# Adapters in float16 halves, turned by DMA and normalised in two fused VectorE passes

## The reference

```python
x = x + cross_attention(x, f)        # 16 heads of 32, keys/values from x, plus one "self" score per query
x = x + softmax((f' + bias) @ f.T) @ f         # layer 1: one head over 512 features
# layer 2, per sample one of 10 adapters
h = relu(x @ W1 + b1); y = x + h @ W2 + b2
x = x + (y - mean(y)) * rsqrt(var(y) + 1e-5) * gamma + beta
# layer 3, per sample one of 4 low-rank pairs
x = x + (x @ A.T) @ B.T + emb
```

## Time and profile before

| | |
|---|---|
| time, median of 3 runs | 1299.4 us (1297.53 to 1302.03) |
| the profiled execution | 1299.96 us; its span 1298.2 us; mean granted PE clock 0.991 |
| busy share of the span | PE 97%, DVE 66%, ACT 65%, POOL 38% |
| one sample | 156.2 us from one mid stage to the next |

### The profile page before, as it was taken

One profiled execution on the slowest core, in us unless ns is written; L12 is line 12 of the kernel. 1 busy time (PEld: TensorE's weight loads), 2 busy tenths in 40 slices (PEclk: granted clock), 3 DMA queues, 4 the chain that ended last, 5 costly groups with the idle time before them and its releaser, 6 DMA issues.

```text
span 1298.2 us, 19231 instructions
## 1 busy us (share of the span) xinstructions
PE 1258.6 (97%) x6697; PEld 523.2 (40%) x6697; DVE 860.6 (66%) x1561; ACT 848.3 (65%) x1795; POOL 489.5 (38%) x428
## 2 busy tenths in 40 slices
PE   7899999999999999999999999999999999999996
PEld 4332454325543344433544245442454324543243
DVE  5976449764697547974389743886449855597544
ACT  4898349873598636985379753888439873598631
POOL 6414344143632246321553416514244143532024
PEclk9999999999999999999999999999999999999996
DMA  6303532135223152242521334213442136222020
GB/s 216 72 16 108 108 69 70 56 91 109 50 65 106 53 98 63 52 125 47 97 62 50 116 74 82 55 53 108 93 77 62 43 98 127 52 66 89 5 33 33
DMA packets 156142, 98.85 MB, mean 76 GB/s; under 512 B 107338, under 2 KB 130182, under 8 KB 156046
## 3 DMA queue, kind: packets, MB, share of 16 engines
q1 hardware_dynamic: 155984, 97.61, 31.1%
q10 hardware_dynamic: 62, 0.01, 0.0%
HBM read 40.81 MB, written 8.40 MB: 38 GB/s over the span
## 4 chain that ended last, share of the span: by engine, by line
PE 70%; DVE 14%; ACT 13%; issue 2%; POOL 1%; ACTq 0%; POOLq 0%; DVEq 0%
PE bank L476 24%; PE banks L476 13%; PE banks L1441 8%; PE bank L1457 8%; DVE nmx L1093 7%; ACT banks L814 6%; PE banks L1376 4%; ACT big L865 4%; PE bank L1278 3%; PE bank L1404 2%; PE bank L1409 2%; PE bank L1431 2%; PE bank L1467 1%; DVE y L1051 1%; ACT bank L894 1%
## 5 line engine op out<-in xcount | busy, mean ns | idle before, releaser
L814 ACT ACTIVATE banks<-banks,nmx 128x512 f32<-128x512 f32 x512 | 341.7, 685 | 41.6 <-DVE nmx L1093 39.4
L1093 DVE TENSOR_REDUCE nmx<-banks 128x1 f32<-128x512 f32 x512 | 328.8, 686 | 16.9 <-PE banks L1376 16.0
L865 ACT ACTIVATE big<-banks 128x1024 f32<-128x1024 f32 x256 | 248.0, 1021 | 54.4 <-PE banks L1441 53.4
L476 PE MATMUL bank<-fT,w_hi 128*128 128x512 f16 x768 | 255.7, 379 | 0.7 <-DVE fT L1007 0.6
L1376 PE MATMUL banks<-KQ 97*128 97x512 f16 x512 | 195.8, 382 | 11.0 <-ACT banks L814 10.8
L1441 PE MATMUL banks<-KQ 98*128 98x512 f16 x512 | 143.5, 383 | 3.6 <-ACT big L865 0.2
L476 PE MATMUL bank<-fT,w_lo 128*128 128x512 f16 x384 | 145.4, 379 | 0.0
L511 POOL TENSOR_TENSOR half<-qk,ones 128x512 f16<-128x512 f32 x64 | 66.7, 1042 | 206.4 <-ACT qk L796 197.9
L511 POOL TENSOR_TENSOR split<-tiles_in,ones 128x512 f16<-128x512 f32 x56 | 60.4, 1079 | 222.3 <-DMA xT<-split 206.2
L1457 PE MATMUL bank<-big,V 128*32 128x512 f32 x1024 | 136.4, 605 | 0.0
L586 POOL TENSOR_TENSOR x<-x,bo_rows 128x512 f32<-128x512 f32 x32 | 40.1, 1286 | 208.1 <-DMA x<-in_x_dram 208.1
(11 more groups left out here) (154 smaller groups left out, 1821.4 us busy)
## 6 DMA issues: line engine op xcount, KB each, us to landing
KQ<-half SPq DMA_DIRECT2D x384, 64.0 KB, 2.0
tiles_in<-in_x_dram SPq DMA_DIRECT2D x32, 256.0 KB, 7.7
x<-in_x_dram SPq DMA_DIRECT2D x8, 1024.0 KB, 5.9
out_dram<-x SPq DMA_DIRECT2D x32, 256.0 KB, 2.0
tiles_in<-in_fside_BxSxS_dram SPq DMA_DIRECT2D x28, 256.0 KB, 3.7
w<-in_L_cond_W_dram SPq DMA_DIRECT2D x16, 256.0 KB, 4.7
b2r<-in_L_cond_b_dram SPq DMA_DIRECT2D x8, 256.0 KB, 4.6
gr<-in_L_cond_gamma_dram SPq DMA_DIRECT2D x8, 256.0 KB, 5.5
```

The costliest lines, as they stand in the source:

```text
L476: mm = eng.matmul(out_ap, pairs[n][0], pairs[n][1], start=(first and n == 0), stop=(last and n == len(pairs) - 1))
L814: eng.activation(bank(step, i)[:, v, :], bank(step, i)[:, v, :], ACT.Exp, bias=nmx[:, t, h:h + 1], accum_out=esum[:, t, h:h + 1]).then_inc ...
L865: eng.activation(big[:, n % 2, 2 * u:2 * u + 2, :], bank(step)[:, :, :], ACT.Exp).then_inc(read(step), 1)
L1093: eng.tensor_reduce(nmx[:, t, h:h + 1], bank(step, i)[:, v, :], AX_X, ALU.max, negate=True).then_inc(max_done, 1)
```

## The change

Layers 2 and 3 are computed in float16 halves in place of float32. In the seven mid stages x1 is split into a high half (ACT) and a low half (DVE) and turned by SP's DMA transposes (steps `X2`, in place of `X2T`); after the normalisation POOL splits x3 (`X3`) and SP turns it (`T3`). `HID` and `LOW` then work on a pair of tiles (256 tokens): 12 and 8 float16 matmuls of 128x256. `LORA` is one float16 matmul. W1 is split by POOL in the attention stage (`split_w1`). The normalisation is two DVE operations for each tile: `U` (`centre`: (y - mean) times gamma) and `SCALE` (`scale`: times 1/sqrt, plus x1 + beta); POOL does no part of it but x1 + b2 and x1 + beta as before. y of all four tiles has room of its own (`tiles_in`), so that all `ADP` can run early. The table `at` gives the slots (entry n stands in slot 2n). After sample 7 the transposes by PE stay, with halves (ACT high, DVE low). The small tables are made earlier in the attention stage, on DVE.

```diff
@@ order_mid: the adapters' places @@
-        adapters = [("X2T", 0), None, ("HID", 0), None, ("ADP", 0), None, ("X2T", 1), ("SQ", 0), ("HID", 1), ("ADP", 1),
...
+        at = {2: [("HID", 0)], 3: [("ADP", 0)], 4: [("SQ", 0), ("ADP", 1)], 5: [("SQ", 1), ("HID", 1)],
+              6: [("U", 0), ("ADP", 2)], 7: [("U", 1), ("SQ", 2), ("ADP", 3)], 8: [("SQ", 3)], 9: [("U", 2)], 10: [("U", 3)],
+              11: [("SCALE", 0)], 12: [("SCALE", 1)], 14: [("X3", 0)], 15: [("X3", 1)], 16: [("SCALE", 2), ("T3", 0)],
+              17: [("SCALE", 3), ("X3", 2), ("T3", 1)], 18: [("X3", 3)], 21: [("T3", 2)], 22: [("T3", 3)],
+              24: [("LOW", 0)], 25: [("LORA", 0)], 27: [("LORA", 1)], 29: [("LOW", 1)], 31: [("LORA", 2)], 33: [("LORA", 3)]}
+        for n in range(NORM_PIECES):
+            at[8 + n // 2] += [("NORM", 0, n)]
+            at.setdefault(13 + n // 2, []).append(("NORM", 2, n))
...
-    out, later = [], {}
+    out, later = [("X2", t) for t in range(NT) if tail], {}
@@ POOL @@
-                    elif step[0] == "SCALE":
+                    elif step[0] == "X3":
                         t = step[1]
-                        eng.wait_ge(normed, i * NT + t + 1)
-                        eng.tensor_tensor(y[:, t % 2, :], y[:, t % 2, :], gr[:, :], ALU.mult).then_inc(scaled, 1)
-                        eng.wait_ge(scaled, i * NT + t + 1)
-                        eng.wait_ge(xg_done, i * NT + t + 1)
-                        eng.tensor_tensor(x1[:, t, :], y[:, t % 2, :], x1[:, t, :], ALU.add).then_inc(x3_done, 1)
+                        eng.wait_ge(x3_done, i * NT + t + 1)
+                        eng.wait_ge(x2t_in[t // 2], i * 32 + 32)
+                        split(p16[:, t, 0:S], p16[:, t, S:2 * S], x1[:, t, :], x3_hi, i * NT + t + 1, x3_lo)
@@ SP @@
+                    elif step[0] == "X2":
+                        t = step[1]
+                        eng.wait_ge(x2_lo, i * NT + t + 1)
+                        turn(aT2, t, p16[:, t, :], x2t_in[t // 2])
+                    elif step[0] == "T3":
+                        t = step[1]
+                        eng.wait_ge(x3_lo, i * NT + t + 1)
+                        turn(aT2, t, p16[:, t, :], x3t_in[t // 2])
@@ ACT @@
+                    elif kind == "X2":
+                        t = step[1]
+                        wait_read(eng, ("PV1", t), i)
+                        eng.activation(p16[:, t, 0:S], x1[:, t, :], ACT.Copy).then_inc(x2_hi, 1)
@@ DVE @@
+            def centre(t, i):
+
+                eng.wait_ge(sq_done, i * NT + t + 1)
+                eng.scalar_tensor_tensor(out=yb[:, t, :], in0=yb[:, t, :], scalar=st[:, t, 1:2], in1=gr[:, :],
+                                         op0=ALU.add, op1=ALU.mult).then_inc(normed, 1)
+
+            def scale(t, i):
+                eng.wait_ge(newton, i * (NT // 2 * NEWTON) + t // 2 * NEWTON + NEWTON)
+                eng.wait_ge(normed, i * NT + t + 1)
+                eng.wait_ge(xg_done, i * NT + t + 1)
+                eng.scalar_tensor_tensor(out=x1[:, t, :], in0=yb[:, t, :], scalar=st[:, t, 4:5], in1=x1[:, t, :],
+                                         op0=ALU.mult, op1=ALU.add).then_inc(x3_done, 1)
...
+                    elif kind == "X2":
+                        t = step[1]
+                        eng.wait_ge(x2_hi, i * NT + t + 1)
+                        eng.tensor_tensor(p16[:, t, S:2 * S], x1[:, t, :], p16[:, t, 0:S], ALU.subtract).then_inc(x2_lo, 1)
@@ PE @@
                     elif kind == "HID":
+                        at = tokens(step, head)
...
+                        if head:
+                            eng.wait_ge(x2t_in[step[1]], i * 32 + 32)
...
+                        hi_lo(eng, bank(step, i)[:, 0:at.stop - at.start], [(w1[:, 0, d, :], w1[:, 1, d, :]) for d in range(ND)],
+                              [(aT2[:, 0, d, at], aT2[:, 1, d, at]) for d in range(ND)]).then_inc(done(step, i), 1)
...
                     elif kind == "LOW":
+                        at = tokens(step, head)
+                        if head:
+                            eng.wait_ge(x3t_in[step[1]], i * 32 + 32)
```

More of the change, by code:

```diff
@@ L83, in order_mid @@
     if tail:
-        n0, n2 = ([("NORM", t, n) for n in range(NORM_PIECES)] for t in (0, 2))
-        adapters = [("X2T", 0), None, ("HID", 0), None, ("ADP", 0), None, ("X2T", 1), ("SQ", 0), ("HID", 1), ("ADP", 1),
[L86 to L92, removed]
+        at = {2: [("HID", 0)], 3: [("ADP", 0)], 4: [("SQ", 0), ("ADP", 1)], 5: [("SQ", 1), ("HID", 1)],
[3 rows of a table added]
+              24: [("LOW", 0)], 25: [("LORA", 0)], 27: [("LORA", 1)], 29: [("LOW", 1)], 31: [("LORA", 2)], 33: [("LORA", 3)]}
+        for n in range(NORM_PIECES):
+            at[8 + n // 2] += [("NORM", 0, n)]
+            at.setdefault(13 + n // 2, []).append(("NORM", 2, n))
+        adapters = [at.get(n, []) for n in range(max(at) + 1)]
     slots = (parts(("K", 0)) if tail else [("IN", NT), ("IN", NT + 1), *parts(("K", 0))[:2], ("IN", NT + 2), *parts(("K", 0))[2:4],
@@ L134, in order_mid @@
     assert rows and i >= max(later)
-    return out + [a for a in adapters if a] + ([] if sums else [("SROW",)])
+    return out + [a for each in adapters for a in each] + ([] if sums else [("SROW",)])
 OPEN = ((32, 26, 26, 26), (24, 24, 24, 24))
@@ L208, in order_last, with tokens @@
             + [("X2T", 0), ("HID", 0), ("X2T", 1), ("PV1", 2), ("ADP", 0), ("HID", 1), ("SQ", 0),
-               ("PV1", 3), ("ADP", 1), ("SQ", 1), ("X2T", 2)] + norm[0]
+               ("PV1", 3), ("ADP", 1), ("U", 0), ("SQ", 1), ("X2T", 2), ("U", 1)] + norm[0]
             + [("HID", 2), ("X2T", 3), ("SCALE", 0), ("HID", 3), ("X3T", 0), ("SCALE", 1), ("ADP", 2), ("LOW", 0),
-               ("X3T", 1), ("SQ", 2), ("ADP", 3), ("LOW", 1), ("SQ", 3)] + norm[2]
+               ("X3T", 1), ("SQ", 2), ("ADP", 3), ("LOW", 1), ("U", 2), ("SQ", 3), ("U", 3)] + norm[2]
             + [("LORA", 0), ("LORA", 1), ("SCALE", 2), ("X3T", 2), ("SCALE", 3), ("LOW", 2), ("X3T", 3),
                ("LORA", 2), ("LOW", 3), ("LORA", 3)])
-ADAPTER_STEPS = set(order_mid(True, False))
+ADAPTERS = ("X2", "X2T", "HID", "ADP", "SQ", "U", "NORM", "SCALE", "X3", "T3", "X3T", "LOW", "LORA")
+def tokens(step, head):
+    n = NT // 2 if head else 1
+    return slice(step[1] * n * P, (step[1] + 1) * n * P)
 def plan_banks():
@@ L596, in _ @@
             add_bo(B - 1)
-            mid(True, False, B - 1, [step for step in order_last() if step in ADAPTER_STEPS])
+            split_w1(B - 1)
+            mid(True, False, B - 1, [step for step in order_last() if step[0] in ADAPTERS])
         @block.sync
```

295 lines of the change are left out of this document (177 added, 118 removed).

## The result

The changed kernel takes 1418.3 us (median of 4 runs, 1412.6 to 1424.1) against 1298.9 us: the ratio is 1.0913, with a 95% interval from 1.0892 to 1.0934. The forecast was 1378 us, with 1314 to 1408. The direction and the two waits were right; the loss is 119 us and not 79.

What follows compares the result with a forecast made beforehand. PE alone bounds the mid stage before the first maximum and in the tail; between, PE, ACT and DVE are nearly full. Per stage +18.3, -7.7 and clock 1.2 make +11.8: 1299.96 + 83 - 5 = 1378 us, range 1314 to 1408 (80%).

Steps and rivals of the forecast that it cites:

- attention and layer 1: Attention stage: charged nothing, W1's split (3.5 us) lying on POOL while it waits for data.
- PE's saving ahead of slot 35: Mid stage before the first maximum: new steps on PE cost about what the old did, so 0 saved.
- The first wait: PE at HID 0, slot 4: waits 4.7 us for the DMA-turned tiles (bounds 3.2 to 5.4).
- The second wait: First maximum on DVE: chain of 11.3 us plus some 11 us hold-up by POOL; first exponential at 675.7 against 657.38.
- What the rest gives back: Mid stage from first exponential to attention: 53.9 us in place of 61.6, so 7.7 us gained per stage.
- 0.5 of gaps: First to last exponential: ACT's idle time, taken as 0.5 us on top of 49.5 us of work.
- The clock: PE's lower clock after its two idle times in a mid stage: 0 to 2 us each, 1.2 us in all.
- After sample 7: Behind the last mid stage: 5 us gained (bounds -10 and 0), with POOL's SCALE gone and LORA in float16.
- That DVE and POOL hardly hold each other up: Rival, DVE's chain: first exponential at 664.7, 1314 us; half the hold-up gives 1329; together 15%.
- LOW 0 waiting 6 us for the turned tiles: Within a rival, slot 48: PE waits 6 us as T3 1 lands at 677.0; +2.7 us per stage.
- That the work taken off PE is simply gained: Rival, mid stages: 7 us gained in each, 1246 us; 7% for all times under 1296.
- The rival of the clock that stays down longer: Rival, PE's two idle times: 2 us at each, ADP chain equally late, +16 per stage, 1407 us; with all worse, 8%.

Runs made afterwards that it cites:

- hid_late: Changed kernel with HID 0 in slot 14 in place of slot 4 and the steps behind it closer together, same work: 1391.9 us.
- pool_small: Changed kernel with POOL doing 8 of 512 columns in its operations beside DVE's chain, so results differ from the reference: 1338.0 us.
- add_early: Changed kernel with POOL's four x1 + beta moved right behind its x1 + b2, where DVE idles: 1391.2 us.
- fill_second: Changed kernel with 48 repeated first matmuls of K 2 on PE ahead of K 2's own, filling PE's second idle time: 1403.8 us.
- low_tail: Changed kernel with LOW and LORA of the mid stages behind the last maximum, same work: 1422.8 us (two runs).
- the two fills: Changed kernel with repeated matmuls in PE's idle time, each run by itself: 20 ahead of the first HID, 1403.6 us; 48 ahead of K 2, 1403.8 us.
- newton_once: Changed kernel with one Newton chain of 15 steps for four tiles in place of two chains, x1 + beta at its start: 1415.3 us.
- spread3: Changed kernel with HID 0 later, one Newton chain, earlier x1 + beta, SCALE behind first maxima, later LOW and LORA: 1294.5 us, ratio 0.9966 to the kernel before.

## Why the forecast was right and where it failed

Profiled against profiled execution, 124.1 us are lost, where the forecast had 78. By its own steps:

| | forecast | measured in the profiles |
|---|---|---|
| K 0 to first exponential, 7 stages | 7 x 18.3 | 7 x 19.4 |
| the rest of the mid stage | 7 x -7.7 | 7 x -2.4 |
| the clock, charged apart | 7 x 1.2 | in the two rows above |
| attention and layer 1 | 0 | 7 x -0.3 |
| the start, up to sample 0's attention | 0 | +6.1 |
| after sample 7 | -5 | +0.5 |
| outside the span | 0 | +1.0 |

Some 5 us of the start are in the profiled execution alone. Between medians the loss is 119 us, 41 more than forecast.

**PE's saving ahead of slot 35: 0.** Nearly right: of the 28.18 us busy up to the first exponential the low clock has 2.5 and what follows the first scores 2.8, which leaves 22.9; before, 22.12. In hid_late, where PE hardly waits there, the first score comes 22.9 to 23.1 us after K 0. So PE has some 0.8 us more to do there than before.

**The first wait.** Right in place and size: HID 0 at 6.8 (6.8 forecast), 4.4 us (4.7). hid_late removes it.

**The second wait.** Right: 21.3 us of chain (22.3), 11.5 without POOL (11.3), so 9.8 us of hold-up for the forecast's 11, shown by pool_small from one side and by add_early from another. The first exponential came 1.1 us later than the forecast's 675.7 has it without the clock.

**"What the rest gives back": this is the step that failed.** It gave 7.7 us and measures 2.4; 7 x 5.3 = 37 of the 46 us that the sum is short. ACT's work was nearly right (49.96 for 49.5). The term that was mis-sized is its "0.5 of gaps": it is 4.6 us. No row gave 0.5. The window of before that the forecast read, 55.53 us with ACT busy 52.07, has 3.5 us of gaps, and it has them in each of the seven stages; the forecast took these for room that PE's saving would win back ("ACT allows 55.5 - 52.1 = 3.4 us"). The runs show that they are none: with LOW and LORA among the maxima, at full clock too (fill_second 3.8), ACT idles at least as long as before the change. So 3 of the 4.1 us that are missing stood in the kernel before, and about 1 came with the change. By cause, 2.6 of the 4.6 belong to LOW and LORA (low_tail) and 0.8 to the clock (fill_second), each shown by itself; beyond the forecast's 0.5 another 0.7 are left over and no run tells whose they are, nor what makes the 3.5 of before. My reading of why the gaps stay, which no run tests by itself: PE needs 0.65 us from one score to the next (719.63, 720.28) and ACT 0.66 from one exponential to the next (740.88, 741.54), so PE hardly wins back a lead of four maxima that is once spent, and each later wait of DVE or PE reaches ACT. The other 0.7 us are in the stretch from the last exponential to attention, 4.54 for 3.85.

**The clock.** The mechanism was right, the size too small: 1.2 us per stage were forecast, and the two fills get 3.7 back in the mid stages, 2.2 and 1.5 (bounds: 0 to 2 for each wait). In the sum ahead of the first exponential it did no harm, and that is luck: the chain was taken 1.0 us too long, and this with the 1.2 charged apart covers the 2.2 of the first wait.

**After sample 7.** -5 was wrong by 5.5 us. The first SCALE starts at 84.45 us from the attention stage's start, where POOL's second operation stood at 83.74: the pass that was saved went to steps that now stand before it (U 0, U 1, the low halves); which of them takes how much I have not taken apart. PE waits 5.92 us for SCALE 2 as it waited 6.07 before.

**The start** was in no part of the forecast, and is no effect of the change: see the last section.

**The rivals.** That DVE and POOL hardly hold each other up is refuted by pool_small. Its price, LOW 0 waiting 6 us for the turned tiles, was real once F came down (newton_once, 5.20 us). That the work taken off PE is simply gained is refuted; even spread3, without either wait, gains 4 us of 49. The rival of the clock that stays down longer (1407 us) came nearest to the time, and had its 2 and 2 us nearly right (2.2 and 1.5); but it kept the 0.5 of gaps too.

## What to carry to other kernels

Where one engine hands work to another through a few buffers at nearly the same pace, do not count the idle time that one of them shows as room: ACT's 3.5 us per stage were taken for 3 us to gain, and 4.6 were measured. When work is moved from the full engine to an idle one, place it by what stands behind it there: nearly the same operations (in the last three with one Newton chain in place of two) gave 1418, 1304 and 1295 us in three orders, and 1398 in one that differs from the last by the slots of two turns, of LOW and LORA and of a piece of Newton. A table of slots has to be moved together with the queue (SP's here) that feeds it.

## What the runs showed of the hardware

One DVE operation can lose to two POOL operations in a row. At the start of the profiled execution a cast of 128x8 values, which takes 0.17 to 0.57 us in all thirteen other profiles, took 6.28 us, until the second of two MEMSETs ended, and what stands behind it came later (timeline, first microseconds):

```profile
6.46 3.51 POOL L537 MEMSET KQ<- 32x4096 f32 x1
...
7.16 6.28 DVE L987 CAST vec<-cols 128x8 f16<-128x8 f32 x1
...
9.91 3.51 POOL L538 MEMSET KQ<- 32x4096 f32 x1
```

In the thirteen other profiles, twelve of them with the same start of the program, the cast began at 5.5 to 6.1, ahead of the first MEMSET. Sample 0's attention starts at 99.5 us here and at 91.7 to 93.4 in the thirteen others, which is enough for the 5.8 us between the profiled run and the median. So this is the luck of one execution, in which the cast came 1.1 us or more later. The hold-up is also not only that of operations with two inputs: the TENSOR_SCALAR of line 1092 has one, and took 1.20 beside 0.17 us. The Trainium skill ("SBUF — State Buffer", "Who interferes with whom") lists casts and `tensor_scalar` among those that can enter a mode with both ports and then block; these rows agree as to the blocking, though none shows the mode in which they ran, while the sentence of it on which the forecast leaned names two inputs alone. TensorE after an idle time of 4.5 us ran 5.9 us at the granted clock 0.57, after 11 us idle 5.0 us at 0.51: 2.5 us lost in each case. Here the shorter of the two waits cost as much clock as the longer.
